# One drive product on VectorE for two scan units in a four-layer convolution and attention hybrid

## The reference

```python
delta = jax.nn.softplus(dt @ dt_w + dt_b)
dA = jnp.exp(delta[..., None] * A)
dBx = delta[..., None] * Bm[:, :, None, :] * xc[..., None]
def comb(a, b):
    return (a[0] * b[0], b[0] * a[1] + b[1])
hstates = jax.lax.associative_scan(comb, (dA, dBx), axis=1)[1]
y = jnp.einsum('blds,bls->bld', hstates, Cm) + Dp * xc
```

## Time and profile before

| what | value |
|---|---|
| median of 3 runs | 4808.23 us (4807.68 to 4814.56) |
| the profiled execution, its own time | 4805.23 us |
| its span, first to last instruction | 4803.0 us |
| mean granted TensorE clock | 0.952 |
| busy: TensorE / VectorE / GpSimd / ScalarE | 4174.5 / 3672.0 / 2602.1 / 2355.4 us |
| scans (L588) | 1536, 1949.7 us busy |
| drive products (L575) | 1536, 1042.4 us busy |

### The profile page before, as it was taken

One profiled execution on the slowest core, in us unless ns is written; L12 is line 12 of the kernel. 1 busy time (PEld: TensorE's weight loads), 2 busy tenths in 40 slices (PEclk: granted clock), 3 DMA queues, 4 the chain that ended last, 5 costly groups with the idle time before them and its releaser, 6 DMA issues. The chain is left out here.

```text
span 4803.0 us, 44678 instructions
## 1 busy us (share of the span) xinstructions
PE 4174.5 (87%) x13922; PEld 1785.6 (37%) x13922; DVE 3672.0 (76%) x4698; ACT 2355.4 (49%) x3553; POOL 2602.1 (54%) x2084
## 2 busy tenths in 40 slices
PE   6899999999999999999998999860998889888964
PEld 2333333333333333333333333320555546555643
DVE  4999999999999999999999999985105425414335
ACT  5566666666566666666666666631103222212223
POOL 4788888888788888888788888760000000000000
PEclk8999999999999999999999999995999999999976
DMA  3444444444444444444444444332202020000000
GB/s 98 131 131 134 133 135 132 130 135 136 134 131 136 131 138 132 128 135 133 136 131 135 132 133 133 120 117 55 57 4 54 4 58 17 9 23 4 17 0 14
DMA packets 135880, 462.01 MB, mean 96 GB/s; under 512 B 20783, under 2 KB 23282, under 8 KB 133822
## 3 DMA queue, kind: packets, MB, share of 16 engines
q1 hardware_dynamic: 135646, 459.18, 32.0%
HBM read 433.64 MB, written 20.97 MB: 95 GB/s over the span
## 5 line engine op out<-in xcount | busy, mean ns | idle before, releaser
L664 POOL TENSOR_TENSOR prod<-states,c_rows 128x512 f32<-128x512 f32 x1536 | 1953.4, 1285 | 466.7 <-DVE states L588 439.1
L588 DVE TENSOR_TENSOR_SCAN states<-decay,carry,bpsum 128x512 f32<-128x512 f32 x1536 | 1949.7, 1269 | 0.0
L354 PE MATMUL ypsum<-prod,identity 128*128 128x512 f32 x3072 | 1595.0, 600 | 0.1
L455 ACT ACTIVATE decay<-delta,decay_rate 128x512 f32<-128x512 f32 x1536 | 1075.8, 715 | 810.4 <-DVE states L588 669.4
L575 DVE TENSOR_TENSOR bpsum<-bpsum,dx 128x512 f32<-128x512 f32 x1536 | 1042.4, 679 | 31.1 <-POOL dx L682 26.6
L347 PE MATMUL bpsum<-b_rows,select 96*128 96x512 bf16 x1536 | 598.6, 390 | 236.7 <-DVE states L588 236.3
L354 PEld LDWEIGHTS ypsum<-prod,identity 128*128 128x128 f32 x3072 | 595.7, 196 | 282.1 <-issue 213.6
L347 PEld LDWEIGHTS bpsum<-b_rows,select 96*128 96x128 bf16 x1536 | 147.8, 96 | 1198.1 <-DVE states L588 808.9
L1066 PE MATMUL convp<-img_hi,w_hi 96*96 96x512 f16 (+1 forms) x1568 | 482.8, 385 | 59.3 <-PEq L1444 43.1
L1414 DVE SCALAR_TENSOR_TENSOR x<-convp,unscale,x_group 96x1024 f32<-96x1024 f32 x16 | 20.4, 1278 | 406.3 <-PE convp L1066 406.3
L1066 PE MATMUL convp<-img_hi,w_lo 128*96 128x512 f16 (+1 forms) x896 | 276.0, 387 | 0.0
(11 more groups left out here) (217 smaller groups left out, 4593.4 us busy)
## 6 DMA issues: line engine op xcount, KB each, us to landing
c_rows<-c_map SPq DMA_DIRECT2D x512, 512.0 KB, 3.7
c_rows<-c_map SPq DMA_DIRECT2D x512, 256.0 KB, 3.9
x_in<-in_x SPq DMA_DIRECT2D x16, 384.0 KB, 5.8
fused_map<-fused SPq DMA_DIRECT2D x16, 384.0 KB, 5.1
work<-fused_map SPq DMA_DIRECT2D x4, 1536.0 KB, 9.5
x<-in_x SPq DMA_DIRECT2D x4, 1536.0 KB, 15.7
x_biased_map<-work SPq DMA_DIRECT2D x4, 1536.0 KB, 7.1
x_group<-x_biased_map SPq DMA_DIRECT2D x16, 384.0 KB, 3.8
```

The lines of the kernel that those rows point to most:

```text
L354: pe.matmul(ypsum[:, group % Y_BANKS, :], identity[:, :], prod[:, n % P_RING, :], start=s == 0, stop=s == STATES - 1).then_inc(summed, 1)
L455: act.activation(decay[:, n % RING, :], delta[k % 2][:, g, :], ACT.Exp, scale=decay_rate[:, ORDER[k][0], g, s:s + 1]).then_inc(decay_ready, 1)
L588: dve.tensor_tensor_scan(states[:, n % H_RING, :], decay[:, n % RING, :], bpsum[:, n % B_BANKS, :], carry[:, at, u:u + 1], ALU.mult, ALU.a ...
L664: pool.tensor_tensor(prod[:, n % P_RING, :], states[:, n % H_RING, :], c_rows[:, n // C_STATES % C_RING, n % C_STATES, :], ALU.mult).then_ ...
```

## The change

VectorE makes the drive product for two units in one instruction: 1024 columns over two neighbouring B banks, with `dx` read twice by a broadcast dimension. It is issued in each odd slot t for units t+1 and t+2. It waits for both broadcasts and counts two on `scaled`. TensorE issues its broadcasts in pairs: in each even slot t those of units t+4 and t+5, at the place in the slot where one stood. `B_LEAD` goes from 3 to 4; there are still four B banks, and each broadcast still waits until the unit that had its bank is scanned.

```diff
@@ -27,7 +27,7 @@
 H_RING, P_RING, RING = 8, 8, 5
 B_BANKS, Y_BANKS = 4, 2
 SUM_LAG = 5
-B_LEAD, DECAY_LEAD = 3, 4
+B_LEAD, DECAY_LEAD = 4, 4
 C_STATES, C_RING = 2, 4
@@ -434,8 +434,9 @@
                 for t in slots:
                     w, at, coming, done, _ = now(t)
-                    if 0 <= t + B_LEAD < UNITS:
+                    if 0 <= t + B_LEAD < UNITS and t % 2 == 0:
                         broadcast_b(t + B_LEAD)
+                        broadcast_b(t + B_LEAD + 1)
                     if done is not None:
                         epilogue(w, at, done)
                     if 0 <= t - SUM_LAG < UNITS:
@@ -566,14 +567,15 @@
-                def scale_unit(n):
+                def scale_two(n):
                     k, u = divmod(n, STEP_UNITS)
                     g, s = divmod(u, STATES)
                     if s == 0:
                         dve.wait_ge(dx_ready, 3 * k + g + 1)
-                    dve.wait_ge(b_full, n + 1)
-                    dve.tensor_tensor(bpsum[:, n % B_BANKS, :], bpsum[:, n % B_BANKS, :], dx[k % 2][:, g, :],
-                                      ALU.mult).then_inc(scaled, 1)
+                    dve.wait_ge(b_full, n + 2)
+                    two = bpsum[:, n % B_BANKS:n % B_BANKS + 2, :]
+                    dve.tensor_tensor(two, two, dx[k % 2][:, g, :].unsqueeze(1).to_broadcast([128, 2, CHUNK]),
+                                      ALU.mult).then_inc(scaled, 2)
@@ -642,8 +644,8 @@
                 for t in slots:
                     w, at, coming, done, current = now(t)
-                    if 0 <= t + 1 < UNITS:
-                        scale_unit(t + 1)
+                    if 0 <= t + 1 < UNITS and (t + 1) % 2 == 0:
+                        scale_two(t + 1)
                     if 0 <= t < UNITS:
                         scan_unit(t)
```

## The result

The changed kernel takes 5539.8 us (5538.9 to 5547.8), the kernel before 4809.3: 1.152 times as long, interval 1.150 to 1.154. That is 731 us more; the forecast was 552 more, with 5190 to 5500 as its range. All of it lies in the phase that was changed: its last scan ends at 3953.1 us instead of 3218.1, 735 us later, and what follows takes 1584.7 us (1584.9 before).

What follows compares the result with a forecast made beforehand. The prediction took VectorE, 97% busy, as the bound. To the profiled 4805 us it added 526 us, the waits less the merge's saving, and 30 for the clock: 5361, stated as 5360, range 5190 to 5500.

Steps and rivals of the forecast that it cites:

- slots 8 and 10, residual: In steps closing a layer-0 step, the residual add waits for output, sum, output on TensorE: 1.9 and 2.1 us.
- slot 20, `xc`: VectorE waits 3.7 us for `xc`, after slot 17's last layer-input product and ScalarE's work; before: none, or 1.2 every second step.
- slot 27, `xc2`: VectorE waits 2.3 us for `xc2`, which follows slot 25's TensorE work and ScalarE's copy and tanh.
- slot 36, B's split: VectorE waits 3.6 us, 1.1 before, for the projection of slot 34 and ScalarE's hand-over.
- slot 47, `dx`: VectorE waits 5.0 us, 0.4 before, for the chain from the third dt product through ScalarE and GpSimd.
- the clock term: TensorE's clock falls after idle time, making the pairs of slots 46 and 0 dearer: 1 us a step, 30 us.
- the held order: TensorE's slot work, held behind the pair's second broadcast, makes VectorE wait: 526 us in all, less the merge's saving.
- The rival in which the clock stays low: Clock falls and stays low at slots 20, 36 and 46: 3 to 6 us a step, 5420 to 5510; 16%.
- The merged product: The 1024-column drive product holds VectorE 1.13 us, saving 0.03 us a pair, 0.7 us a step, 23 us over 768 pairs.
- The vector bound: Rival: broadcasts come in time, stage waits stay, only the merge counts: 4785 us, by its bounds 4748 to 4900; 5%.
- That only TensorE's rate counts: Rival: stages have hidden slack, only slots 10 to 17 and 6 to 11 hurt: mean +0.6 us a step, 4830; 4%.
- The half-of-the-waits case: Rival: chains run partly beside each other, so half of the waits appear: 4808+260 = 5070 us; 10%.

## Why the prediction was wrong

**The direction, the place and most of the size held.** TensorE's half, held behind the second broadcast, makes the loss, and moving the pair takes nearly all of it back. Term by term, for the step from 1760.85 to 1883.77 us, one that closes a layer-0 step:

| VectorE waits in | forecast | measured |
|---|---|---|
| slot 5, skip | 1.4 | 1.3 |
| slots 8 and 10, residual | 1.9, 2.1 | 1.7, 2.1 |
| slots 10 to 17, broadcasts | 0.4 | 1.6 |
| slot 20, `xc` | 3.7 | 3.5 |
| slot 22, skip | 0 | 0.6 |
| slot 27, `xc2` | 2.3 | 2.8 |
| slot 36, B's split | 3.6 | 3.5 |
| slots 38 and 29 | 0.4 | 0.2 |
| slots 43 and 45, broadcasts | 0 | 4.6 |
| slot 47, `dx` | 5.0 | 4.2 |
| sum | 20.8 | 26.1 |

The step before it, of the other kind, has 23.7 us of waits against 18.6, again with 4.6 in slots 43 and 45 that the forecast has at nothing.

**The step that failed is the clock term.** The prediction took 1 us a step (30 in all), and put it at slots 46 and 0, after the longest idle stretch. With the clock kept up (0.98), a step takes 115.9 us (1077 scans in 2600 us), 6.3 less than in the changed kernel; the forecast without its clock term came to 115.1. Over the whole phase that run is 557 us longer than the kernel before, the forecast without its clock term was 526, and the changed kernel is 735 longer. So the held order was sized well, and the clock was undersized by a factor of six and put in the wrong place. Slots 46 and 0 are light, as the text said, and there a slow TensorE is absorbed whole. But slots 38 to 41 have the dt products, which head the chain to `dx`, and behind the residual slots stand the first input products:

```profile
1792.84 0.61 PE L347 MATMUL bpsum<-b_rows,select 96*128 96x512 bf16 x1 [1.83 <-DVE states L590]
1793.24 1.91 PE L354 MATMUL ypsum<-prod,identity 128*128 128x512 f32 x2
```

That is the pair of slots 10 and 11; the broadcasts behind it come 1.4 us late in slot 15. The waits for `xc` themselves are not the clock's: 131.1 us with it kept up, 132.4 without. The forecast looked for the longest idle time; it should have looked for the idle time that stands ahead of the fullest slots.

Both the price and the warning stood in the trace of the kernel before. Its row behind the broadcast of the earlier trace rows is a product of 512 columns at 1.91 us, where the same lasts 1.02 at full clock; and the earlier trace rows are not the only slow ones. In the very step that the prediction reads, TensorE's clock falls in slot 41 after 0.99 us of idle time:

```profile
80.70 1.91 PE L382 MATMUL mm<-x_in,center_w 96*96 96x512 f32 x2
...
1539.18 0.61 PE L347 MATMUL bpsum<-b_rows,select 96*128 96x512 bf16 x1 [0.99 <-DVE states L588]
1539.58 1.91 PE L354 MATMUL ypsum<-prod,identity 128*128 128x512 f32 x2
```

The granted clock of 1539 to 1541 us is 0.55. It cost nothing there, since the dt products were done. The rival in which the clock stays low, 3 to 6 us a step with 5420 to 5510, was the right case, and its top was still 30 us short. I gave it 16%.

**The merged product** was right: a product 1.219 us long, which holds VectorE 1.11 (start 1853.24, scans from 1854.37 there: 1.13; 1.11 where nothing waits) against the forecast 1.13. The Trainium skill's (N+151)/0.96 ns ("VectorE: DVE Perf Modes", The TRN2 errata) gives 1224 ns, and the trace agrees on the length. It doesn't bear out that a merge saves the fixed part of that rule, 0.157 us: by start-to-start rows it saves 0.03 to 0.06 us a pair.

**The rivals.** The vector bound did not hold. That only TensorE's rate counts was wrong for the changed kernel, but it is what is left of it when the order is mended: 4872 and 4883 us, 62 and 75 us slower than before, all of it waits for broadcasts and `dx`. The half-of-the-waits case was wrong: in the table each wait is there at nearly its full size. The reason that I see, each wait moves the scan behind which TensorE's next work is held, is argued and not tested.

## What to carry to other kernels

A wait blocks everything behind it on its queue. When an instruction with a late condition is moved ahead, or doubled, cost the work behind it first; here the same pair behind the slot's work instead of ahead of it was worth 656 us of 731. With a fixed number of buffers a longer lead does not fetch earlier, it waits later. And where an engine's waits grow on TensorE, look at the granted clock in the slots that follow, not only at the idle time itself: the price depends on what stands there.

## What the runs showed of the hardware

TensorE's clock fell after short idle stretches too, and not after all of them. In the changed kernel 2.25 us of idle time (1853.44 to 1855.69) left it at 0.99, and 2.05 us soon after were followed by 12 us at 0.50, in which TensorE was busy 98% of the time. But one stretch alone did it as well: from 1792.84 to 1814.54 no row of TensorE has idle time before it, and then came

```profile
1816.67 0.61 PE L347 MATMUL bpsum<-b_rows,select 96*128 96x512 bf16 x1 [2.13 <-DVE states L590]
```

with a granted clock of 0.57 over the next 3.8 us. Over the phase of the changed kernel all 30 broadcasts behind 5 us and more of idle time were slow, and 58 of the 139 behind 1.75 to 2.75 us; in the kernel before 6 of the 69 behind 0.9 to 1.1 us. What decides between them these runs do not show, so a forecast has to count such a stretch as one that may cost.

Copies of a broadcast, work without any use, kept the clock at 0.98 from 400 to 3000 us and took 171 us off. I had not expected either that redundant matmuls could be worth 3% of a kernel or that 5.5 us of idle time in another slot would cost nothing at all.
